# Reordering the opening of two attention layers and the start of the expert loads in a four-layer transformer kernel

## What is computed

```python
x = x + attention0(layernorm(x))   # 32 query heads of 128, 8 key/value heads, rotary embedding, causal softmax
x = x + ffn0(layernorm(x))         # silu(x@gate.T) * (x@up.T) @ down.T, 1792 wide
x = x + attention1(layernorm(x))   # 32 heads of 16, bias on q, k, v, ALiBi slopes, causal softmax
x = x + experts(layernorm(x))      # 64 rank-16 experts, the best 16 of a router, softmax gates
```

## Time and profile before

| | |
|---|---|
| median of 3 runs | 1507.58 us (1506.67 to 1507.61) |
| the profiled execution | 1505.23 us, of which the span from first to last instruction is 1503.2 us |
| PE busy, PEld busy | 1433.1 us (95%), 1195.1 us (80%) |
| DVE, ACT, POOL busy | 1009.5 (67%), 857.5 (57%), 555.7 us (37%) |
| mean granted TensorE clock | 0.991 |
| DMA moved | 71.97 MB |

### The profile page before, as it was taken

The page is one execution under the profiler, slowest core; times in us unless marked ns, Lnnn a source line. Parts: engine busy times, 40 slices in busy tenths (PEclk is TensorE's granted clock), DMA queues, the critical chain, the costliest instruction groups (busy, mean ns, idle before and its releaser), DMA issues.

```text
span 1503.2 us, 25443 instructions
## 1 busy us (share of the span) xinstructions
PE 1433.1 (95%) x7696; PEld 1195.1 (80%) x7696; DVE 1009.5 (67%) x2538; ACT 857.5 (57%) x2184; POOL 555.7 (37%) x484
## 2 busy tenths in 40 slices
PE   5899999999999999999988999999789999988999
PEld 4788888888888888888867888888567777776787
DVE  7776667766777667666656333344688889889742
ACT  2676566655566556665653332220589989988310
POOL 5474464644645456454240000023161314116500
PEclk9999999999999999999999999999899999999999
DMA  4010110100100001000021111114434435461000
GB/s 171 8 50 15 29 43 21 28 21 28 35 21 28 28 28 35 14 28 7 1 71 43 63 60 45 42 36 78 75 84 76 96 69 102 78 144 57 1 22 35
DMA packets 37517, 71.97 MB, mean 48 GB/s; under 512 B 4993, under 2 KB 5377, under 8 KB 36865
## 3 DMA queue, kind: packets, MB, share of 16 engines
q1 hardware_dynamic: 29664, 55.35, 11.8%
q0 software_dynamic: 7776, 15.73, 7.1%
HBM read 60.58 MB, written 10.49 MB: 47 GB/s over the span
## 4 chain that ended last, share of the span: by engine, by line
PE 80%; ACT 6%; DVE 6%; issue 4%; DMA 2%; POOL 1%; DVEq 0%; ACTq 0%; SPq 0%; POOLq 0%
PE ps_up L66 9%; PE ps_up L65 9%; PE ps_up L64 9%; PE ps_gate L64 8%; PE ps_gate L66 8%; PE ps_gate L65 8%; PE ps_out L64 5%; PE ps_out L66 5%; PE ps_out L65 5%; PE ps_out L556 4%; PE ps_up L1853 2%; ACT a_probs L2123 2%; PE ps_out L1841 2%; PE ps_gate L1828 2%; ACT a_probsT_hi L2132 2%
## 5 line engine op out<-in xcount | busy, mean ns | idle before, releaser
L822 ACT ACTIVATE a_probs<-a_probs,a_least 128x512 f32<-128x512 f32 (+3 forms) x256 | 143.0, 560 | 162.2 <-DVE a_least L683 157.2
L405 POOL TENSOR_TENSOR a_rotated<-a_by_cos,a_by_sin 128x512 f32<-128x512 f32 x80 | 103.7, 1296 | 224.9 <-DVE a_by_sin L706 222.7
L691 DVE TENSOR_TENSOR a_probsT_lo<-ps_out,a_probsT_hi 128x512 fp32r<-128x512 f32 (+3 forms) x256 | 118.5, 484 | 67.9 <-ACT a_probsT_hi L830 66.7
L830 ACT CAST a_probsT_hi<-ps_out 128x512 fp32r<-128x512 f32 (+3 forms) x256 | 101.5, 427 | 92.4 <-PE ps_out L556 91.6
L2123 ACT ACTIVATE a_probs<-a_probs,a_least 128x128 f32<-128x128 f32 (+3 forms) x256 | 142.2, 560 | 3.4 <-issue 1.6
L1992 DVE CUSTOM_DVE_ANT_0 a_probs<-ps_gate,a_causal 128x128 f32<-128x128 f32 (+3 forms) x256 | 117.1, 486 | 33.6 <-PE ps_gate L1828 20.7
L882 ACT ACTIVATE a_probs<-a_probs,a_inverse 128x128 f32<-128x128 f32 (+3 forms) x256 | 123.1, 553 | 9.6 <-DVE a_inverse L724 8.6
L415 POOL TENSOR_TENSOR a_query_lo<-a_rotated,a_query_hi 128x512 fp32r<-128x512 f32 x64 | 82.7, 1292 | 107.8 <-ACT a_query_hi L842 107.8
L683 DVE CUSTOM_DVE_ANT_0 a_probs<-ps_out,a_causal 128x512 f32<-128x512 f32 (+2 forms) x192 | 101.2, 551 | 29.6 <-PE ps_out L66 29.6
L64 PE MATMUL ps_up<-a_wo_hi,a_attended_hi 128*128 128x512 f32 x278 | 113.4, 408 | 2.3 <-issue 1.4
L64 PE MATMUL ps_gate<-xT_hi,a_wq_hi 128*128 128x512 f32 x256 | 108.9, 425 | 1.6 <-DVE a_values_lo L719 1.6
(11 more groups left out here) (279 smaller groups left out, 4082.5 us busy)
## 6 DMA issues: line engine op xcount, KB each, us to landing
a_raw<-in_wq SPq DMA_DIRECT2D x36, 256.0 KB, 2.7
a_raw<-in_wo SPq DMA_DIRECT2D x36, 256.0 KB, 2.6
a_stacked_q<-a_spill_q POOLq DMA_DIRECT2D x48, 128.0 KB, 4.5
a_stacked_k<-a_spill_k POOLq DMA_DIRECT2D x24, 256.0 KB, 4.6
f_raw<-in_gate SPq DMA_DIRECT2D x14, 256.0 KB, 2.7
f_raw<-in_up SPq DMA_DIRECT2D x14, 256.0 KB, 2.9
f_raw<-in_down SPq DMA_DIRECT2D x14, 256.0 KB, 3.5
a_raw<-in_wk SPq DMA_DIRECT2D x12, 256.0 KB, 2.8
```

The costliest lines, as they stand in the source:

```text
L691: nc.vector.tensor_tensor(probsT[1][:, t % 2, 0:w], ps_turn[:, t % 2, 0:w], probsT[0][:, t % 2, 0:w].bitcast(F32), ALU.subtract).then_inc( ...
L822: nc.scalar.activation(tile, tile, ACT.Exp, bias=least[:, slot, i:i + 1], scale=-1.0, accum_out=total[:, slot, i:i + 1]).then_inc(exp_done, 1)
```

## The change

Four edits. On GpSimd, all weight splits but the first wait until four tiles have been normalised. On VectorE, the second half's inversion and its four normalisations go behind the rotation of the first keys. In the last projection before chunk 0 of attention1 (query, s = 14) `split_operand` goes one step later, behind the masks. On SP, the expert loads wait until all stacked keys have landed.

```diff
         for c, (what, which) in enumerate(FIRST_PIECES[:SLOTS]):
+            if c == 1:
+                pool.wait_ge(m.ln_semaphores[LN_SEMAPHORES.index("normal_done")], QT)
             split(c, c, 1, what, which)
...
         norm.shift(dve, 1)
-        norm.invert(dve, 1)
-        for t in range(QT, NT):
-            norm.normalise(dve, t)
         dve.wait_ge(consts_in, 16 * 6)
...
         rotate(-1, 4, "keys")
+        norm.invert(dve, 1)
+        for t in range(QT, NT):
+            norm.normalise(dve, t)
         rotate(-1, 5, "query")
...
         sp.wait_ge(keys_out, 2 * 16 * 2 * CHUNKS1)
+        sp.wait_ge(stacked_k_in, 16 * DMAS_K * 2 * CHUNKS1)
         moe.fetch_down(sp, (0, 1))
...
-            if side1 in ("query", "keys") and isinstance(c1, int) and c1 < 0:
+            if side1 in ("query", "keys") and isinstance(c1, int) and c1 < 0 and s1 < STEPS1 - 2:
                 split_operand(c1, s1)
-            if side2 in ("query", "keys") and not (isinstance(c2, int) and c2 < 0):
+            if side2 in ("query", "keys") and not (isinstance(c2, int) and c2 < 0 and s2 < STEPS1 - 2):
                 split_operand(c2, s2)
```

## The result

The changed kernel takes 1499.82 us (median of 7 runs, 1495.88 to 1501.71) against 1506.67 us for the kernel before (7 runs, 1503.83 to 1507.70). The ratio is 0.9956 with a 95% interval of 0.9944 to 0.9967: 6.6 us faster, 5.0 to 8.4. The forecast was 1499.0 and faster, its sum 8.6 us. The total came out near it; the terms did not each.

What follows compares the result with a forecast made beforehand. TensorE was taken to bound the kernel, 80% of the chain, with gains only where it and the pacing engine idle together. Terms 0.4 + 4.3 + 3.9 = 8.6 us, from the median 1507.58, gave 1499.0 us; range 1495.5 to 1503.5.

Steps and rivals of the forecast that it cites:

- the forecast's own three places: The opening, the step before attention1's chunk 0, and attention1's end: gains of 0.4, 4.3 and 3.9 us.
- the four signs of being wrong: Waits at the next unit's mask or on stacked keys, chunk 0's division above 3.10 us, GpSimd waiting for the router.
- The opening: First normalisations and key rotation: an earlier query rotation gains 0.4 us, between 0 and 1.1; ends -1.3 and 2.1.
- The query split: Step before attention1's chunk 0: split behind the masks removes ScalarE's two idle times, 4.3 us gained (3.3 to 4.8).
- the division's 2.7 us stall: Attention1's chunk 0: VectorE's division meets GpSimd's output bias run, 3.10 us instead of 0.43; the forecast let this stand.
- The expert loads: Attention1's end: waiting loads let the last keys land in time, removing TensorE's stall, 3.9 us gained (2.8 to 5.6).
- the quiet case: Keys' read-back at attention1's end: the same DMA one sequence earlier, without loads beside it, takes 5.2 us, not 12.7.
- keys late anyway: Attention1's end: the write or read-back itself sets the keys' landing, so the last term is nothing; 1502.9 us, chance 7%.
- the stall that only moves: Step before chunk 0: ScalarE's rounding comes still later and the next unit's masks wait; 1503.3 us, chance 4%.
- the long run on VectorE: Chunk 0: GpSimd's bias run lengthens the division's stall by up to 8.4 us; 1499.0 to 1507.4 us, chance 8%.
- nothing came slower: Chunk 0: second sequence's keys, read back behind the query's read-back, stall TensorE; 1510.6 us at 14.2 us lateness, chance 3%.
- The rule that spoke against the opening's move: Opening: by port sharing alone the keys' low part always blocks the third normalisation, making this term 0, 0.4 us less.

Runs made afterwards that it cites:

- experiment 3: The opening's two edits on the kernel before: together 1502.38 us against 1505.95; GpSimd's wait alone 1508.30 and the moved normalisations alone 1505.84, both against 1505.06.
- the opening alone: The kernel before with only GpSimd's wait and VectorE's moved inversion and normalisations: 1502.38 us against 1505.95, ratio 0.9982.
- the second profile of the change: The changed kernel, nothing altered, timed and profiled once more against the kernel before: median 1499.99 us against 1506.03, ratio 0.9965.
- pauses alone: The changed kernel with GpSimd waiting on its own previous addition between the eight output bias additions: 1499.65 us against 1505.95 for the kernel before.
- with the additions moved: The changed kernel with GpSimd's eight output bias additions put behind chunk 0's four weight splits: 1493.47 us against 1506.03 for the kernel before.

## Why the prediction was right

The time fell within the range, by the forecast's own three places, but the sum of 8.6 was 2 us too high. That the total came out within 1 us is in part luck: the median that it was counted from, 1507.58 of three runs, lay 0.9 above the 1506.67 of seven. Of the four signs of being wrong that the prediction named, one came: the division in chunk 0 above 3.10 us.

- **The opening** was put at 0.4 us. At the ScalarE row of experiment 3 the two profiles of the change are 0.4 and 0.7 us ahead of the one profile of before, which looks as forecast. But two other profiles with the opening of before reach that row 1.2 us later than this one, so the agreement is no confirmation; all profiles together give 1.4, and the opening alone timed 2.7. Its own profile is 2.3 ahead, as much as the upper end of 2.1, though its normalisations did not miss GpSimd's work. What the step left out is the clock. A hole of 3.81 us before query 6 was followed by a stretch at 0.66 that cost the first score more than query 6 had gained, and the slow stretch that the kernel before has from 44 to 49 us stayed away.
- **The query split** was put at 4.3. The wait, TensorE's stall and ScalarE's idle time went, and 4.8 us was saved up to the division, the upper end. The failing step is the one that let the division's 2.7 us stall stand and made its growth a rival with 8%: it grew by 2.0 us (5.08 for 3.10), because the run's start, tied to the keys' read-back as that rival said, moved by only 1 us in the change's profile while the division moved by 3. 2.8 to 3.0 was kept.
- **The expert loads** were put at 3.9. 4.2 was saved (the DMA landed 5.3 and 5.4 us after its issue, as estimated from the quiet case) and 1.1 given back at the next division, which the prediction did not see: a shift of 0.15 us against GpSimd's splits.
- In the second profile of the change the three terms, each against the one profile of before, are 0.7 + 3.0 + 3.4 = 7.1 of the 8.0 us between these two executions (1505.23 and 1497.27); the measured gain is 6.6. The three parts timed alone add to 8.9, each uncertain by about 1.8; that they add to more than the whole is within these intervals and stays open.
- The rivals: keys late anyway and the stall that only moves did not happen; the long run on VectorE happened, and cost 2.0 us of its 8.4; nothing came slower.

The rule that spoke against the opening's move (the Trainium skill, SBUF — State Buffer, Who interferes with whom: whoever issues first holds the shared ports for the whole instruction) agrees with the two orders of the opening: 2.96 us with VectorE first, 3.74 with GpSimd first. The same section of the Trainium skill says that a VectorE instruction with two inputs in SBUF contends with GpSimd's reads; the division is one, and 0.47 against 5.23 us agrees that they contend. The measured wait goes further than one instruction, though: the division stood over four of GpSimd's. The row of before, 3.10 instead of 0.43, already showed the meeting, so its growth could have been a term of the sum and not a rival.

## What to carry to other kernels

When a wait is removed, look on the other engines for what the freed engine will meet sooner: here a VectorE division with both inputs in SBUF met GpSimd's stream twice, once for 2 us more because it came 3 us sooner, once because of a shift of 0.15 us, and returned two fifths and a quarter of what had been saved. A stall may hide the next one, so follow the queue behind the long instruction (pauses alone moved TensorE's wait from the mask to the weight split), and move work that nobody needs soon behind work that somebody waits for. One profile of such a kernel can sit 2 to 4 us from the median: take terms between two rows of one trace, look at the same two rows in every other version that the edit does not touch, and take the verdict from repeated runs.

## What the runs showed that was not expected

A VectorE instruction held up by GpSimd need not get in at the next instruction's end: the division stood through the last three of the run's additions and the first instruction of the next split, some 4.8 us, and got in where GpSimd paused some 0.1 us on its own semaphore, between the two halves of that split. That pause is not the whole rule: with the additions moved, the query's low part met the same run near its end and took 1.09 us instead of 0.69 without any such pause. What tells the two apart was not tried.

The same program showed a granted clock of 0.57 and of 0.79 from 1056 to 1072 us in two profiles, a place that no edit touches. TensorE's wait of 2.8 to 4.0 us for the first slope DMA of attention1, just before it, is in all of these profiles and was left as it is.
